# A recurrent attention kernel: later reciprocals, an earlier residual sum, and a reordered up tile and key projection

## The reference

```python
qkv = (norm(x) @ W_qkv.T).reshape(B, L, 3, H, dk)
k = (k - mean(k)) / sqrt(var(k) + eps)          # per head
F = retention * F + coef * outer(v_t, k_t)      # for each token
y_t = (W_LTM + F) @ q_t
x = x + norm(y @ W_o.T)                         # first residual
h = square(relu(norm(x) @ W_fc.T)); y = h @ W_proj.T
spikes = number of the 5 steps in which the unit fires
x = x + norm(spikes / 5)                        # second residual
```

## Time and profile before

| | |
|---|---|
| median of 3 runs | 570.86 us (570.71 to 573.21) |
| the profiled execution | 573.23 us |
| its span, first to last instruction | 571.4 us |
| mean granted TensorE clock | 0.914 |
| TensorE busy | 478.8 us, 84% of the span |
| VectorE busy | 514.7 us, 90% |
| ScalarE busy | 366.4 us, 64% |
| GpSimd busy | 385.7 us, 67% |
| VectorE idle ahead of the reciprocals of L945 | 32.6 us |
| ScalarE idle ahead of copies of v, q, yf, attention output, keys | 29.4, 25.1, 27.5, 13.3, 17.4 us |

### The profile page before, as it was taken

The page is one execution under the profiler, slowest core; times in us unless marked ns, Lnnn a source line. Parts: engine busy times, 40 slices in busy tenths (PEclk is TensorE's granted clock), DMA queues, the critical chain, the costliest instruction groups (busy, mean ns, idle before and its releaser), DMA issues.

```text
span 571.4 us, 7792 instructions
## 1 busy us (share of the span) xinstructions
PE 478.8 (84%) x2245; PEld 318.6 (56%) x2252; DVE 514.7 (90%) x746; ACT 366.4 (64%) x901; POOL 385.7 (67%) x206
## 2 busy tenths in 40 slices
PE   4683587759999798979898999989997989897992
PEld 2451244426576566736574657656674657465881
DVE  5799999999997999899897999899989998797767
ACT  4561323664677977887768887896879736863331
POOL 1138978687848977696868795888679694783022
PEclk9686557858989999999899999999999989999997
DMA  7475577457484559547774749454934588410002
GB/s 263 130 205 145 147 208 197 147 148 186 135 215 96 149 124 278 146 130 184 216 196 124 177 114 276 143 145 118 285 109 125 153 244 217 111 39 7 30 2 73
DMA packets 54778, 87.64 MB, mean 153 GB/s; under 512 B 5456, under 2 KB 19408, under 8 KB 54736
## 3 DMA queue, kind: packets, MB, share of 16 engines
q1 hardware_dynamic: 54160, 87.12, 56.3%
q10 hardware_dynamic: 576, 0.03, 0.1%
HBM read 78.74 MB, written 8.39 MB: 152 GB/s over the span
## 4 chain that ended last, share of the span: by engine, by line
PE 59%; DVE 15%; issue 9%; ACT 9%; POOL 5%; DMA 1%; SPq 0%; DVEq 0%; ACTq 0%; POOLq 0%
PE p_c L382 15%; PE p_c L412 12%; DVE state L982 8%; PE p_a L312 7%; PE p_y L360 7%; PE p_c L373 6%; POOL prod L1250 4%; PE p_a L333 3%; ACT sign L713 2%; PE p_y L351 2%; PE p_u L552 1%; ACT oo L615 1%; DVE p_u L972 1%; PE p_a L342 1%; DVE yf L1202 1%
## 5 line engine op out<-in xcount | busy, mean ns | idle before, releaser
L1250 POOL TENSOR_TENSOR prod<-state,qf 128x1024 f32<-128x1024 f32 x127 | 300.3, 2380 | 117.6 <-PE p_y L360 69.3
L982 DVE TENSOR_TENSOR_SCAN state<-ret,p_u 128x512 f32<-128x512 f32 x256 | 308.7, 1209 | 0.0
L972 DVE TENSOR_TENSOR p_u<-vrep,p_k 128x512 f32<-128x512 f32 x256 | 171.5, 676 | 0.1
L382 PE MATMUL p_c<-wproj_sb,ht 128*128 128x256 f32 x448 | 100.4, 379 | 0.0
L382 PEld LDWEIGHTS p_c<-wproj_sb,ht 128*128 128x128 f32 x448 | 84.0, 190 | 12.0 <-ACT yf L626 0.8
L312 PE MATMUL p_a<-xt,wqkv_s 128*128 128x512 f32 x276 | 84.8, 448 | 3.0 <-POOL xt L1266 1.6
L412 PE MATMUL p_c<-x1t,wfc_s 128*128 128x512 f32 x324 | 81.6, 398 | 1.8 <-ACT hr L697 1.1
L360 PE MATMUL p_y<-prod,summer 128*32 128x512 f32 x512 | 73.9, 652 | 9.1 <-POOL prod L1250 8.0
L312 PEld LDWEIGHTS p_a<-xt,wqkv_s 128*128 128x128 f32 x276 | 54.9, 208 | 42.1 <-issue 15.5
L412 PEld LDWEIGHTS p_c<-x1t,wfc_s 128*128 128x128 f32 x324 | 59.3, 188 | 22.8 <-issue 7.3
L713 ACT ACTIVATE sign<-yf,drive_sb 128x512 bf16<-128x512 f32 x60 | 38.1, 709 | 0.2
(11 more groups left out here) (190 smaller groups left out, 614.7 us busy)
## 6 DMA issues: line engine op xcount, KB each, us to landing
vrep<-v_rows SPq DMA_DIRECT2D x256, 256.0 KB, 4.7
xa<-in_x SPq DMA_DIRECT2D x9, 512.0 KB, 4.8
v_rows<-vf SPq DMA_DIRECT2D x16, 256.0 KB, 2.5
x<-in_x SPq DMA_DIRECT2D x7, 512.0 KB, 6.8
out<-x SPq DMA_DIRECT2D x7, 512.0 KB, 3.3
ht<-in_w_fc SPq DMA_DIRECT2D x1, 1024.0 KB, 7.6
wproj_sb<-in_w_proj SPq DMA_DIRECT2D x1, 1024.0 KB, 10.3
state<-in_w_qkv SPq DMA_DIRECT2D x1, 512.0 KB, 6.0
```

What stands on the lines that cost most here:

```text
L382: last = pe.matmul(p_c[(u + 1) % 2][:, 0:D], ht[:, f, tokens(u)], wproj_sb[:, f, :], start=(f == 0), stop=(f == FT - 1))
L972: v.tensor_tensor(p_u[n % NU][:, :], vrep[:, n % NV, :], p_k[:, :], ALU.mult).then_inc(S["hebb_done"], 1)
L982: v.tensor_tensor_scan(state[:, s % NS, i, :], ret[:, r:r + 1].broadcast_to([P, L]), p_u[n % NU][:, :], 0.0, ALU.mult, ALU.add).then_inc(S ...
L1250: p.tensor_tensor(prod[:, s % NZ, :, :], state[:, s % NS, :, :], qf[:, s // HS, :].unsqueeze(1).broadcast_to([P, 2, L]), ALU.mult).then_in ...
```

## The change

VectorE: `scales(1, b)` moves from slot 3 to the end of slot 4, `scales(3, b1)` from ahead of the products of slot 8 to behind the first scan of that slot. GpSimd: `add_attention` moves from slot 6 to slot 5, ahead of one read. TensorE: `project_k(b, 0)` follows `project_v(b, 0)` directly in slot 10, the key variance of slot 11 goes ahead of up(1), up(7) moves from slot 15 into slot 1 of the next iteration, behind the key projection and ahead of the key variance, and the second half of the normed residual is turned in `p_c[0]` instead of `p_a`. ScalarE: `squares_x1` and `deviation(3)` move from slot 7, behind the third copy of yf and the key copy, to slot 6, ahead of both; the signs are cut in two groups, 1 and 4 for the first pair, 2 and 3 for the second; the squares of the keys move to slot 10, `squares_count(b2, 0)` behind them, `key_deviation` ahead of hidden(0), and hidden(7) behind `square_k` of slot 1. The last reload of x gets a semaphore of its own.

```diff
-                        sp.dma_start(xa[:, :, :], by_tile(x, LAST)).then_inc(S["again_in"], 16)
+                        sp.dma_start(xa[:, :, :], by_tile(x, LAST)).then_inc(S["last_in"], 16)
...
             def project_v(b, half):
-                if half == 0: pe.wait_ge(S["x1t_done"], at(KT * (b - 1)))
+                if half == 0: pe.wait_ge(S["x1t_done"], at(KT * (b - 1) - 1))
...
             def count_spikes(b, pair):
+                if pair == 1: pe.wait_ge(S["x1t_done"], KT * (b + 2))
...
             def turn_x1(b, t):
-                pe.wait_ge(S["x1t_done"], at(KT * b + t))
+                pe.wait_ge(S["x1t_done"], at(KT * (b - 1) + t + 1))
+                if t == 1: pe.wait_ge(S["yf_done"], at(TILES * b))
+                bank = p_a if t == 0 else p_c[0]
                 for u in range(TILES):
-                    last = pe.transpose(p_a[:, tokens(u)], oo[:, u, t * P:(t + 1) * P], ident_sb[:, :])
+                    last = pe.transpose(bank[:, tokens(u)], oo[:, u, t * P:(t + 1) * P], ident_sb[:, :])
...
                         if s == 1: project_k(g, 1)
+                        if s == 1 and two_before: up(b2, 7)
...
-                        if s == 10: project_v(b, 0)
-                        if s == 11: project_k(b, 0)
+                        if s == 10:
+                            project_v(b, 0)
+                            project_k(b, 0)
...
                         if s == 11:
+                            key_variance(b, 0)
                             up(b1, 1)
-                            key_variance(b, 0)
                             up(b1, 2)
...
-                        if s == 15:
-                            up(b1, 6)
-                            up(b1, 7)
+                        if s == 15: up(b1, 6)
...
-                        if two_before:
-                            hidden(b2, 6)
-                            hidden(b2, 7)
+                        if two_before: hidden(b2, 6)
                     if s == 1:
                         if now: square_k(g, 1)
+                        if two_before: hidden(b2, 7)
...
-                            signs(b2, 0)
+                            signs(b2, 0, 0, 1)
                     if s == 6:
+                        if before:
+                            squares_x1(b1)
+                            deviation(3, b1)
                         if two_before: copy_yf(b2, 2)
                     if s == 7:
                         if now: copy_key(g)
-                        if before:
-                            squares_x1(b1)
-                            deviation(3, b1)
                         if after: copy_xt(b, 0)
+                        if two_before: signs(b2, 0, 1, 4)
...
-                        if two_before: signs(b2, 1)
-                        if two_before and after: squares_count(b2, 0)
+                        if two_before and after: signs(b2, 1, 0, 2)
+                        if two_before and not after: signs(b2, 1)
                     if s == 10:
                         if after: copy_v(b, 0)
+                        if two_before and after: signs(b2, 1, 2, 3)
+                        if after: square_k(b, 0)
                         if two_before and after:
+                            squares_count(b2, 0)
                             total_count(b2, 1)
...
-                        if after: square_k(b, 0)
                         if two_before and after: deviation(4, b2)
-                        if before and after: hidden(b1, 0)
                         if after: key_deviation(b, 0)
-                        if before and after: hidden(b1, 1)
+                        if before and after:
+                            hidden(b1, 0)
+                            hidden(b1, 1)
...
-                    if before and s == 8: scales(3, b1)
...
-                    if after and s == 3: scales(1, b)
                     if now and s == 4: key_reciprocal(g, 1)
+                    if after and s == 4: scales(1, b)
                     if before and s == 5: scales(2, b1)
                     if now and s == 6: norm_k(g, 1)
+                    if before and s == 8: scales(3, b1)
...
-                dve.wait_ge(S["again_in"], 16 * B)
+                dve.wait_ge(S["last_in"], 16)
...
-                    if before and s == 6: add_attention(b1)
+                    if before and s == 5: add_attention(b1)
```

More of the change, by code:

```diff
@@ L164, in build @@
         S = {name: sem(name) for name in """
-            x_in wv_in wkq_in params_in tables_in weights_in again_in out_done
+            x_in wv_in wkq_in params_in tables_in weights_in again_in last_in out_done
             setup_ready setup_exp wv_high wv_low wk_high wk_low wq_high wq_low wide_high wide_low
@@ L690, in copy_x1t @@
                 act.wait_ge(S["x1t_low"], at(KT * (b - 1) + t + 1))
-                copy(p_a[:, :], x1f[:, t, :], "x1_turned", KT * b + t + 1, "x1t_done")
+                copy((p_a if t == 0 else p_c[0])[:, :], x1f[:, t, :], "x1_turned", KT * b + t + 1, "x1t_done")
                 copy(x1f[:, t, :], x1t[:, 0, t, :], "x1t_done", KT * b + t + 1, "x1t_high")
@@ L707, in copy_yf, with signs @@
                 copy(p_c[(u + 1) % 2][:, 0:D], yf[:, u, :], "down_done", TILES * b + u + 1, "yf_done")
-            def signs(b, pair):
+            def signs(b, pair, first=0, count=STEPS):
                 act.wait_ge(S["yf_done"], at(TILES * b + 2 * (pair + 1)))
                 act.wait_ge(S["count_done"], at(2 * (b - 1) + pair + 1))
-                for j in range(STEPS):
+                for j in range(first, first + count):
                     last = nc.scalar.activation(sign[:, pair, j, :, :], yf[:, 2 * pair:2 * pair + 2, :], ACT.Sign,
                                                 bias=drive_sb[:, j:j + 1], scale=BELOW_ONE)
-                last.then_inc(S["sign_done"], 1)
+                if first + count == STEPS: last.then_inc(S["sign_done"], 1)
             def copy_count(b, pair):
```

## The result

The changed kernel took 566.89 us in its profiled execution, against 573.23 us for the kernel before. The ratio to the kernel before is 0.988, with a 95% interval of 0.983 to 0.993: 1.2% faster. Its plain median of four executions is 570.95 us; the ratio leaves out 575.0 and 603.0 us (mean granted clocks 0.919 and 0.808) and so rests on two, and with the 575.0 us counted in the gain would be 0.6%. A second series of six, taken later, gave 565.1 to 576.3 us and a ratio of 0.995 (0.990 to 1.000). So the gain is small, somewhere between 0.5 and 1.2%. The second series alone doesn't tell it from none, and single executions of the changed kernel lie 11 us apart.

The account below looks back on a forecast made before the run. The loop of TensorE, ScalarE and GpSimd was taken as the bound. Terms of -1.6, +3.0 and -1.4 gave 0.0 us; with 1.0 us for the clock, 570.9 became 571.9 us, range 566.0 to 577.5.

Parts of the forecast that it names:

- The bound: Steady iteration: the loop TensorE, ScalarE, GpSimd sets the period; VectorE has about 56.9 us of work and 4 us of waiting.
- Up tile 7: Moved behind slot 1's key projection: hidden(7) delays the copy of y and the output projection, +1.1 us per steady iteration.
- VectorE's new waits: Waits leave the reciprocals of norm 1 and slot 8 for key copy, key product and second reciprocal, same total surplus.
- Slots 9 to 11: From the turned residual to the sixth sums: two banks, split signs and earlier key projection gain 0.5 us an iteration.
- First and last iterations: Iteration 1 and the start of the steady part gain 1.6 us together; iteration 7 gains 1.4 us.
- The sum of the order: Whole execution, without the clock term: -1.6, then +3.0 over five iterations, then -1.4, together 0.0 us.
- The clock: Waits near the output projection, 1.9 and about 1.1 us, may lower TensorE's clock: 1.0 us added, between -2.5 and +7.
- The second rival: Filled wait ahead of the key variance keeps the clock up, no half-clock output projection: -2.5 us, 568.4 us; chance 0.18.
- the third rival: The 1.9 us wait ahead of the eighth sums lowers the clock there: +7 us in three of six iterations, 578 us; chance 0.20.

Follow-up runs that it names:

- Both reciprocal runs: Changed kernel with both reciprocals at their old places on VectorE, 565.5 us; kernel before with only the two reciprocals later, 572.4 us.
- e_up7_back2: Changed kernel with up tile 7 and hidden(7) back in slots 15 and 0, run a second time: 564.9 us, ratio 0.986.
- e_sq_back: Changed kernel with the residual sum back in GpSimd's slot 6 and the residual's squares and deviation back in ScalarE's slot 7: 578.5 us, ratio 1.010.
- e_fill: Kernel before with six unused matmuls behind the key projection of slot 1, from iteration 2 on: 568.6 us, ratio 0.993.
- e_after_fill: Changed kernel with unused matmuls, seven behind slot 0's value projection and four behind slot 2's key variance, from iteration 2 on: 568.1 to 568.7 us.
- e_y_first: Changed kernel with the copy of y ahead of hidden(7) on ScalarE: 560.2 us, ratio 0.977.
- e_sum_late: Changed kernel with the copy of y ahead of hidden(7) and GpSimd's feed-forward sum behind the read of slot 15: 549.2 us, ratio 0.960.
- e_late_y_back: Changed kernel with only GpSimd's feed-forward sum moved behind the read of slot 15, hidden(7) still ahead of the copy of y: 558.9 us.
- e_up7_only: Kernel before with only up tile 7 and hidden(7) moved behind the key projection and the key squares: 578.4 us, ratio 1.008.
- e_after_again: Changed kernel run again unchanged, beside the others on one chip: median 571.5 us (565.1 to 576.3).

## Why the prediction was wrong

**The bound, right.** TensorE, ScalarE and GpSimd set the period, and VectorE's waits only fill up to it. Both reciprocal runs show it.

**Up tile 7, right.** Forecast: wait ahead of the eighth sums 0.44 to 1.9 us, +1.1 us by the copy of y. Measured: 1.77 us, and 1.05 us of wait (1.17 us a period against e_up7_back2).

**VectorE's new waits, right in place.** Forecast for the three places: 1.8 us at the key product, 0.8 to 1.6 at the second reciprocal, the rest at the key copy. Measured: 1.47, 0.45, 2.52. The second reciprocal's wait is below its bounds, and the key copy took what was missing there.

**Slots 9 to 11, right in size**, with one oversight: I costed the split signs at nothing without saying that the early squares make their place. e_sq_back prices that at 1.2 us. And the earlier trace rows come from an iteration in which the clock had fallen there (value projection 2.73 instead of 1.66 us): TensorE's wait ahead of the count is 0.32 us in it, but 1.87 us in the next one. The key projection fits into the second, so the term holds.

**First and last iterations, a little small.** -2.0 for -1.6, and -1.6 for -1.4. The periods came at +0.5 each for +0.6. The sum of the order was forecast at 0.0 and measured at -1.1 us, in one pair of executions whose first term moves by 2 us from one to the next.

**The clock, wrong.** The sum failed at the term "I add 1.0 us for it". The profiled execution of the kernel before holds three half-clock output projections, 5.1 us. The changed kernel's has none, and the 5.1 us make up four fifths of the 6.3 us between the two. Where the sum adds 1.0 us for the clock, this execution got 5.1 us back, and that was in good part luck: the second profile of the same kernel has two such projections. The second rival had the sign, but I took it against the median with one and a half such projections, 2.5 us, and gave it 0.18. 566.9 us lies inside the range given, but the ratio of 0.988 is a clear gain where I forecast none. In the second series the third rival appeared as well (2.84 us for a projection), and the median of that series, 571.5 us, lies at the forecast of 571.9. So the term can't be given as one number for an execution. What is shown: a gap filled with useless matmuls takes 4.7 us from the kernel before. And over all profiles at the usual clock, half-clock output projections stand only where TensorE waits just ahead of the projection or of the key variance in front of it. With that wait (1.05 to 1.44 us, eleven profiles) they are 26 of 66; without it (e_fill, e_after_fill, e_y_first, e_sum_late) they are 0 of 24. What is not settled: why, with the same gap of 1.05 us ahead of it, the output projection was never at half clock in the changed kernel's first profile, in two of six in e_late_y_back, and in three of six in e_up7_only. Their periods differ (61.4, 59.5, 62.0 us), but the period alone doesn't decide, as e_after_again has two of six at 61.4 us.

The Trainium skill, page TensorE: Matmul & The Clock Gate, section Why this matters for your kernels, ties drops of the clock to long gaps without matmuls. Here half-clock stretches on the path began behind gaps of 1.05 to 1.88 us, in some iterations and not in others. The measurement decides: the rule names the right cause, but a gap that it would let pass can cost.

## What to carry to other kernels

Find the loop that sets the period before moving an instruction of an engine that waits: a wait on VectorE moved to another product each time, and only orders inside the loop of TensorE, ScalarE and GpSimd (copy of y, sum on GpSimd, squares and signs) changed the period. When work is moved to fill a gap, follow what its result makes late on the next engine: up tile 7 filled a gap of 1.17 us, which gave nothing, and its relu held the next projection for 1.05 us. And compare two orders at the same clock, period by period, since half-clock stretches of 1.7 us each hid a difference of 0.5 us an iteration.

## What was not expected of the hardware

Matmuls that nobody reads, in TensorE's waits, sped the kernel up: 573.3 to 568.6 us with six of them an iteration (1.4 us) in one gap. The same kernel differs by 11 us between six executions. Two of its profiles agree to 0.03 us in the first three periods, and then only one of them has steps of the granted clock, which start behind gaps of 1 to 2 us; they make its last two periods 1.6 and 3.3 us longer. With two of these gaps filled, four executions differed by 0.6 us, but so small a spread (1.4 us) also came once without filling. One half-clock stretch costs 1.7 us on an output projection (5.39 for 3.70 us) and 1.2 us on a projection of six matmuls (2.84 for 1.65 us).
